# A four-layer convolution network on one Trainium2 core: a closing stage with two normalised tiles and 32-wide products, and a deformable stage normalised on ScalarE

## The reference, cut to what matters

```python
def dsc_axis(x, offset, weight, axis):        # layer 2, once along the rows, once along the columns
    ...
    s = grid_sample_zeros(x, ix, iy)
    return jnp.einsum('bchwk,ock->bohw', s, weight)

def _L3_conv_ref(x, freq_weight):             # layer 3
    kern = _equivariant_kernel(freq_weight)   # (32, 32, 3, 3)
    pad = K // 2
    return jax.lax.conv_general_dilated(x, kern, window_strides=(1, 1), padding=[(pad, pad), (pad, pad)], ...)

x = x + _L2_conv_ref(_gn(x), ...)             # ends in relu(batchnorm(...))
x = x + _L3_conv_ref(_gn(x), L3_conv_freq_weight)
```

## Time and profile before

| what | value |
|---|---|
| median of 3 runs | 4784.35 us (4765.66 to 4795.29) |
| the profiled execution, its own time | 4795.68 us |
| its span, first to last instruction | 4794.0 us |
| deformable stage, from 1992 us of the span on | 2408 us |
| closing stage, from 4407.7 us on | 386.3 us |
| granted TensorE clock, whole span | 0.878 of 2.4 GHz |

### The profile page before, as it was taken

How to read it: one execution, slowest core, us unless ns; L and a number is a source line. 1 busy time by engine, 2 the same in 40 slices (tenths; PEclk the granted TensorE clock), 3 DMA queues, 4 the chain that set the end, 5 groups by cost and what they waited for, 6 DMA issues and landing times. The chain is left out here.

```text
span 4794.0 us, 149995 instructions
## 1 busy us (share of the span) xinstructions
PE 3845.9 (80%) x58786; PEld 2247.2 (47%) x58786; DVE 2727.2 (57%) x5226; ACT 2636.6 (55%) x2855; POOL 2628.0 (55%) x1899
## 2 busy tenths in 40 slices
PE   7765558336999855399999998999989999995688
PEld 5665445232333322255555555555555555553222
DVE  4303646443333334387777777678777787775443
ACT  5500114231222244388778787788878878885332
POOL 0001200011000023499999999999989999997332
PEclk9956669658999977699999999999999999998798
DMA  3365659998777656411232212321223102222753
GB/s 97 72 125 141 190 123 261 266 303 204 215 217 213 182 185 198 79 43 26 58 66 50 55 25 57 65 49 36 49 55 68 46 29 58 54 48 77 162 136 67
DMA packets 663416, 533.27 MB, mean 111 GB/s; under 512 B 34431, under 2 KB 595711, under 8 KB 653855
## 3 DMA queue, kind: packets, MB, share of 16 engines
q1 hardware_dynamic: 544262, 386.05, 33.7%
q10 hardware_dynamic: 108560, 105.02, 7.1%
q0 software_dynamic: 9984, 33.56, 2.1%
HBM read 338.35 MB, written 186.16 MB: 109 GB/s over the span
## 5 line engine op out<-in xcount | busy, mean ns | idle before, releaser
L1576 POOL TENSOR_SCALAR df_t<-df_t 128x1536 f32<-128x1536 f32 x1536 | 2224.7, 1485 | 136.8 <-ACT df_t L1620 114.2
L1793 PE MATMUL df_o<-df_t,df_zs 128*32 128x128 f32 x36864 | 1375.0, 283 | 66.9 <-issue 55.0
L1649 DVE TENSOR_SCALAR df_t<-df_d 128x512 int32<-128x512 int32 x1536 | 1060.5, 690 | 431.2 <-PE df_d L1745 415.4
L1620 ACT ACTIVATE df_t<-df_a 128x1024 f32<-128x1024 f32 x1024 | 1050.0, 1025 | 331.1 <-PE df_a L1745 286.9
L1793 PEld LDWEIGHTS df_o<-df_t,df_zs 128*32 128x32 f32 x36864 | 942.1, 112 | 532.6 <-issue 453.9
L1745 PE MATMUL df_d<-df_ix,net_sel 11*128 11x512 bf16 x1536 | 605.3, 394 | 55.0 <-DVE df_t L1649 45.2
L1620 ACT ACTIVATE df_t<-df_z 128x1024 f32<-128x1024 f32 x512 | 524.8, 1025 | 166.6 <-PE df_z L1745 148.2
L1624 ACT ACTIVATE df_zs<-df_z 128x864 f32<-128x864 f32 x512 | 453.4, 885 | 1.5 <-PE df_z L1771 1.5
L1771 PE MATMUL df_z<-net_Z,df_x 32*128 32x288 f32 x4096 | 409.9, 458 | 0.1
L1745 PE MATMUL df_a<-df_ix,net_sel 11*128 11x512 bf16 x2048 | 406.3, 393 | 0.6 <-DVE df_s L1688 0.5
L1093 POOL CAST of_parts<-of_t_o 128x512 bf16<-128x512 f32 x64 | 39.8, 623 | 649.6 <-ACT of_t_o L1063 649.5
(11 more groups left out here) (231 smaller groups left out, 5001.8 us busy)
## 6 DMA issues: line engine op xcount, KB each, us to landing
gc_x<-x SPq DMA_DIRECT2D x240, 128.0 KB, 4.9
dc_x<-x SPq DMA_DIRECT2D x240, 128.0 KB, 3.2
dc_xt<-x_2t SPq DMA_DIRECT2D x240, 128.0 KB, 4.7
fw_x<-in_x SPq DMA_DIRECT2D x32, 512.0 KB, 6.3
iv_x<-in_x SPq DMA_DIRECT2D x64, 256.0 KB, 4.8
x<-iv_x POOLq DMA_DIRECT2D x64, 256.0 KB, 5.0
y<-gc_o ACTq DMA_DIRECT2D x64, 256.0 KB, 5.8
r_y<-y SPq DMA_DIRECT2D x8, 2048.0 KB, 14.2
```

The lines of the kernel that those rows point to most:

```text
L1576: g.tensor_scalar(t, t, 1.0, 0.0, ALU.min, ALU.max).then_inc(hat_p, 1)
L1620: act.activation(T[:, m % 2, 3 * i:3 * i + 2], src, ACT.Abs).then_inc(a_read, 1)
L1649: v.tensor_scalar(T[:, m % 2, 3 * i + 2].bitcast(I32), ps_d[:].bitcast(I32), 0x7fffffff, None, ALU.bitwise_and).then_inc(d_read, 1)
L1793: mm = pe.matmul(ps_o[32 * q:32 * q + 32, 0:P], Zs[:, m % 2, q, 32 * k:32 * k + 32], T[:, m % 2, 3 * i + x, P * q:P * q + P], start=(k == ...
```

## The change

Closing stage. The normalised image is written twice. XA has it as it lies; XB has groups 0 and 1 at row j and groups 2 and 3 at row j+1, a row of zeros at the free end. XA is written by VectorE in one piece of 4096 numbers, XB by ScalarE in two pieces of 64 partitions x 4096 (`shifted`, as scale * x + shift; the shift is -mean/deviation, two more small steps on VectorE). With these, every output row group q finds its three input rows at one offset: groups 1 and 2 in XA, group 0 in XB at row j, group 3 in XB at row j+1. So a chunk is now 3 x shifts x 4 groups = 12 products, each 128 deep, 32 wide and 512 columns long, into its own 32 partitions of the bank. The halo tiles, their copies on GpSimd and ScalarE and the products with LA and LB are gone; GpSimd only sets the two tiles to zero. The mean product now follows chunk 3, the variance product chunk 4, and on VectorE `mean` follows result 3, `variance` result 4. On ScalarE `activate(b+2)` now follows `shifted(b+1)`, and `send(b,0)` comes ahead of `root(b+1)`. L4 has the taps of all three rows for each group (12 copies), and LA and LB no longer exist.

Deformable stage. The normalising moves from VectorE to ScalarE, as scale * x + shift with the shifts of all images worked out once (NB), in the same lines 10 to 17, behind that line's `distances` and `read_z`; the eight pieces ahead of the loop move too.

The diff, cut to its core:

```diff
-        XN = s.sb("xn", [P, 2, J + 2, W + 2])
-        HA, HB = (s.sb(n, [96, 2, HJ * W]) for n in ("ha", "hb"))
+        XA = s.sb("xa", [P, 2, J, W + 2])
+        XB = s.sb("xb", [P, 2, J + 1, W + 2])
...
-                            g.tensor_copy(HA[32 * x:32 * x + 32, e].rearrange("c (j w) -> c j w", w=W),
-                                          XN[96:128, b % 2, HJ * e:HJ * e + HJ, x:x + W]).then_inc(above, 1)
+                g.memset(XA[:], 0.0).then_inc(set_, 1)
+                g.memset(XB[:], 0.0).then_inc(set_, 1)
...
-                def halo(b, e):
...
+                def shifted(b):
+                    if b == 0:
+                        a.wait_ge(set_, 2)
+                    a.wait_ge(steps, ST * (b + 1))
+                    if b >= 2:
+                        a.wait_ge(conv, NC * (b - 1))
+                    for r, j in ((slice(0, 64), 0), (slice(64, 128), 1)):
+                        a.activation(XB[r, b % 2, j:j + J, 1:W + 1], X[r, b % 3].rearrange("p (j w) -> p j w", w=W), ACT.Identity,
+                                     bias=nm[r, b % 2, 2:3], scale=nm[r, b % 2, 1:2]).then_inc(moved, 1)
...
                 for b in range(B):
+                    send(b, 0)
                     if b + 1 < B:
                         root(b + 1)
-                    send(b, 0)
-                    if b + 2 < B:
-                        a.wait_ge(added, b + 1)
-                        activate(b + 2)
                     send(b, 1)
                     if b + 1 < B:
-                        halo(b + 1, 0)
+                        shifted(b + 1)
+                    if b + 2 < B:
+                        activate(b + 2)
                     send(b, 2)
                     send(b, 3)
-                    if b + 1 < B:
-                        halo(b + 1, 1)
...
-                    for x in range(2):
-                        pe.matmul(bank[:], wt["L4"][:, x, :], XN[:, b % 2, 1 + j:5 + j, x:x + W], start=(x == 0), stop=False)
-                    if c % 4 == 0:
-                        pe.wait_ge(above, 6 * b + 3 * e + 3)
-                        pe.wait_ge(below, 6 * b + 3 * e + 3)
-                    r = slice(512 * (c % 4), 512 * (c % 4) + 512)
-                    pe.matmul(bank[0:32, :], wt["LA"][:], HA[:, e, r], start=False, stop=False)
-                    pe.matmul(bank[96:128, :], wt["LB"][:], HB[:, e, r], start=False, stop=False)
-                    pe.matmul(bank[:], wt["L4"][:, 2, :], XN[:, b % 2, 1 + j:5 + j, 2:2 + W], start=False, stop=True).then_inc(conv, 1)
+                    for x in range(3):
+                        for q in (1, 2, 3, 0):
+                            if q == 3 and x == 0 and c == 0:
+                                pe.wait_ge(moved, 2 * b + 2)
+                            r = slice(32 * q, 32 * q + 32)
+                            t, k = ((XB, j), (XA, j), (XA, j), (XB, j + 1))[q]
+                            mm = pe.matmul(bank[r, :], wt["L4"][:, x, r], t[:, b % 2, k:k + 4, x:x + W], start=(x == 0), stop=(x == 2))
+                    mm.then_inc(conv, 1)
...
# deformable, ScalarE
+                def normalise(b, a, p):
+                    if p == 0:
+                        act.wait_ge(x_in[a], 64 * (b + 1))
+                        alone(act, passed)
+                    xp = X[a][:, 512 * p:512 * p + 512]
+                    act.activation(xp, xp, ACT.Identity, bias=NB[:, bass.ds(b, 1)],
+                                   scale=GS[:, 1, bass.ds(b, 1)]).then_inc(xn, 1)
...
                         if more or m + 2 < ST:
                             ahead_of(*ahead(b, m, 2))
-
+                        if 10 <= j < 18 and (more or a == 0):
+                            normalise(*((b, 1) if a == 0 else (b + 1, 0)), j - 10)
# deformable, VectorE
-                    v.tensor_scalar(xp, xp, GS[:, 0, bass.ds(b, 1)], GS[:, 1, bass.ds(b, 1)],
-                                    ALU.subtract, ALU.mult).then_inc(xn, 1)
```

More of the change, by code:

```diff
@@ L1124, in closing @@
     NC = 8
-    HJ = J // 2
     with Stage(nc, sems, "cl") as s:
@@ L1141, in closing @@
         o_out = [s.sem(f"o_out{k}") for k in range(4)]
-        relu, added, steps, sums, rooted, normed = (s.sem(n) for n in ("relu", "added", "steps", "sums", "rooted", "normed"))
-        above, below, conv, o_done = (s.sem(n) for n in ("above", "below", "conv", "o_done"))
-        ST = 8 + 1 + 1 + 3 + 1 + 1
+        relu, added, steps, sums, rooted = (s.sem(n) for n in ("relu", "added", "steps", "sums", "rooted"))
+        normed, moved, conv, o_done = (s.sem(n) for n in ("normed", "moved", "conv", "o_done"))
+        ST = 8 + 1 + 1 + 3 + 1 + 1 + 2
         with s.block() as block:
@@ L1286, in _ @@
                         stats(b + 1)
-                    result(b, 1)
+                    for c in (1, 2, 3):
+                        result(b, c)
                     if more:
                         mean(b + 1)
-                    result(b, 2)
+                    result(b, 4)
                     if more:
                         variance(b + 1)
-                        normalise(b + 1, 0)
-                        normalise(b + 1, 1)
-                    for c in range(3, NC):
+                        normalise(b + 1)
+                    for c in range(5, NC):
                         result(b, c)
@@ L1424, in _ @@
                     r = slice(32 * q, 32 * q + 32)
[L1425 to L1430 removed]
+                    for y in range(3):
+                        t = (q - y + 1) % 4
+                        v.tensor_copy(wt["L4"][r, :, 32 * t:32 * t + 32], taps[r, y])
             @block.scalar
@@ L1723, in image @@
                             stats(b, par, c)
+                v.tensor_tensor(NB[:], GS[:, 0], GS[:, 1], ALU.mult).then_inc(shift, 1)
+                v.wait_ge(shift, 1)
+                v.tensor_scalar(NB[:], NB[:], -1.0, None, ALU.mult).then_inc(shift, 1)
                 with v.Fori(0, 1) as b:
-                    for p in range(8):
-                        normalise(b, 0, p)
                     for p in range(8):
```

69 lines of the change are left out of this document (22 added, 47 removed).

## The result

The changed kernel takes 4628.85 us (median of 4 runs, 4622.94 to 4634.74), the kernel before 4783.94 beside it (4 runs): the ratio is 0.9667, 95% interval 0.9648 to 0.9686. The profiled execution has a span of 4629.7 us, where before had 4794.0: 164.3 us less.

A forecast was written before the change was run, and what follows sets the result against it. GpSimd was taken to bound the deformable stage and a chain of waits the closing one; closing -107 and deformable -20 (-27 + 7 + 1) sum to -127 us, 4784.35 becoming 4657, range 4612 to 4720.

The forecast's parts named there:

- The head: Closing stage, its start up to the end of image 2's relu, forecast at 4479.8 us on the trace.
- The loop: Closing stage: a loop through ScalarE, addition to root, sends, two shifted writes and relu, sets 30.5 us an image.
- chunk 4 behind the wait: Closing stage: the chunk behind the mean product runs at the low clock after TensorE idles, 5.3 us.
- The chunk of 2.70: Closing stage, TensorE: twelve products as 3 sets x 2 x 0.45 us, four side by side, 2.70 us a chunk.
- first halves: Deformable stage: GpSimd's stalls around VectorE's normalising pieces go, 3.8 us an image, 27 us over images 1 to 7.
- second halves: Deformable stage: lines of 4.55 to 4.7 us against 4.30 (today 4.47), 0.7 to 1.9 us worse an image, 7 taken.
- ScalarE's line of 4.55: Deformable stage: ScalarE's 3.96 us a line plus 0.59 for the normalising piece of 512 columns.
- 60 us to win: Deformable stage, by the skill's port rule: each piece stops GpSimd for half a microsecond, 15 halves x 8 x 0.5.
- Transfers as the bound: Rival, closing stage: a round takes 38 us instead of 30.5, 37 us more, 4694 in all; chance 0.10.
- ScalarE as the bound of the deformable stage: Rival: all 128 pieces show in both halves, +56 us instead of -20, 4733 in all; chance 0.07.
- The low clock: Rival, closing stage: TensorE stays at the low clock, chunk 5.4 us, image 44.1, about 4750 in all; chance 0.05.
- Products not side by side: Rival, closing stage: a chunk takes 10.8 us, an image 87.3, 5118 in all, slower; chance 0.04.

The follow-up runs named there:

- experiment 1: Each stage's change alone: new closing stage with the old deformable function, 4674.7 us; old closing stage with the new deformable function, 4744.27 us.
- close_only: The changed kernel with the whole deformable function of the kernel before, so only the closing stage is changed: 4674.7 us, ratio 0.9758.
- quarters: The changed kernel with each of the 128 normalising pieces on ScalarE as four activations of 128 numbers instead of one of 512: 4709.63 us, ratio 0.9842.
- relu_early: The changed kernel with image b+2's relu issued behind send(b,0), ahead of root and the shifted writes: 4598.86 us, ratio 0.9607.
- relu_send: As relu_early, and send(b,1) also moved behind shifted(b+1): 4591.11 us, ratio 0.9594.
- by_quarter: The changed kernel with a chunk's twelve products reordered, the three x shifts of one group behind each other, then the next group: 4662.0 us, single run.

## Why the prediction was right, and where a term was off

The forecast was 4657 us with a range of 4612 to 4720; 4628.85 lies inside, 28 us below the forecast: -155 us between the medians against -127. Between the profiled spans it was -164.3. That parts into: closing stage -114.6; hats of the loop from first to last 2402.0 to 2346.6, -55.4; the pieces ahead of the loop +1.5; and 4.2 us by which the stages ahead, which the change does not touch, were later. Of the -55.4 some 14 come with the old loop too (experiment 1).

**Closing stage: -107 forecast, -114.6 measured.** The head was right: the relu of image 2 ends 72.0 us into the stage (4430.0), forecast 72.1. The loop had the right members in the right order. Its round was forecast as 30.5; the relus end 27.7, 30.4, 29.2, 29.3 and 30.5 us apart, 29.4 in the mean. The round shown above is the forecast's almost to a tenth: mean product 4556.90 - 4546.66 = 10.24 (10.69), root at 16.96 (17.1), relu's end at 30.4. What differs between rounds is chunk 4 behind the wait, taken as 5.3 each time; behind a wait of 1.84 us it was 2.71, and behind waits of 3.54 us 5.28, 4.04, 4.33, 5.28 and 5.28. Five rounds give 5.4 of the 7.6 us, the last eight chunks (20.9 instead of 22.9) the other 2. The chunk of 2.70 came out as 2.6.

**Deformable stage: -20 forecast, about -54 between the two profiles and -46 between medians, and here is the term that was mis-sized.** In first halves the forecast was -27; lines 12 to 19 lost 298.2 - 266.4 = 31.8 (28.8 against `close_only`). The eight pieces ahead of the loop were forecast at +1 and cost 1.5. The step that failed is "In second halves 4.55 to 4.7 against 4.30 (today 4.47): 0.7 to 1.9 us worse than today an image, seven times, 7 taken". Lines 44 to 51 got 15.0 us shorter (12.6 against `close_only`), 22 from the forecast. Two things are behind it. ScalarE's line of 4.55 was a sum of lengths; by starts the line is 4.32, although the piece itself lasts 0.81 and not 0.59, and `quarters` shows that starts are what count. So the line stayed at GpSimd's pace, 240.5 / 56 = 4.29: 7 x 8 x (4.47 - 4.29) = 10 us. And 4.47 was read from image 3 alone: it holds in five of the seven images (35.7 us for the eight lines), but in images 1 and 2 the first pieces stall GpSimd in second halves too (39.1 and 37.8); these 5.4 us went as well. Two signs that the prediction named did not come: the line of 4.5 to 4.6 us in second halves, and a stage of 2380 to 2395 us, which is 2365.9. A further 8.6 us (of which 7.5 in lines 34 to 43) lie in lines of the loop that the forecast did not treat; kernels with the same loop differ there by as much.

**The two statements on GpSimd and VectorE.** I went by the rows and against the page (the Trainium skill, SBUF — State Buffer, "Who interferes with whom"), by which whoever comes first holds the ports for its whole instruction; my estimate from that was 60 us to win. Measured were 31.8 + 15.0 = 46.8 in the lines with pieces (41.4 against `close_only`), between the two. One new row speaks for the page. VectorE now works out the shifts NB, 8 numbers per partition, while GpSimd sets a tile to zero:

```profile
1950.39 13.75 POOL L1584 MEMSET df_ix<- 128x16384 bf16 x1 [18.41 <-POOLq L1019]
1950.72 0.17 DVE L1713 TENSOR_TENSOR df_nb<-net_GS 128x8 f32<-128x8 f32 x1 [17.87 <-PEq L1019]
1950.92 13.24 DVE L1715 TENSOR_SCALAR df_nb<-df_nb 128x8 f32<-128x8 f32 x1
```

The tensor_scalar of 8 numbers lasts 13.24 us and ends with the memset: it waited for the whole instruction. It costs nothing here, since the loop's first tile is not in before 1984.

**The rivals.** *Transfers as the bound* fell: `relu_early` and `relu_send` make them go faster than after does. *ScalarE as the bound of the deformable stage* fell for after, and `quarters` shows it as it was meant, 0.8 us per line further on. *The low clock* fell as a bound of the whole stage (0.86, up from 0.83); what it costs shows in chunk 4, up to 5.28 us instead of 2.71. *Products not side by side* fell, and even in the order of `by_quarter` three ran side by side.

## What to carry to other kernels

ScalarE, running back to back, is timed by the distance between starts, not by the sum of lengths: here 4.32 against 4.78 us a line, and against a bound of 4.30 that turned a forecast loss into a gain. A product that waits for another engine belongs behind as much independent work as there is: moved ahead by three chunks, it left TensorE idle 11.3 us instead of 3.5 an image and cost 60 us. Behind a wait TensorE can pay a second time (a chunk of up to 5.28 us behind 3.54 us idle, 2.71 behind 1.84). When a chain through one engine is the bound, look at what stands on it without need: moving one relu ahead of two copies, with no change of the work, gave another 30 us, and the best kernel of the study is `relu_send`, 4591.11 us.

## What the runs showed that was not expected

- A VectorE operation of 8 numbers per partition took 13.24 us beside a GpSimd memset of 13.75 us, while another of 0.17 us passed at the memset's start.
- On VectorE neither an odd count (511) nor a stride of two changed the time per number (0.5 ns), and a form with two input tensors (0.75 us for 512) waited beside GpSimd like the others, up to 5.38 us.
- ScalarE needed 0.48 us for 128 numbers and 0.81 for 512, in place and in a row 0.39 and 0.70 apart; 1024 numbers out of PSUM took 1.02 and stood 0.90 apart. A small piece is mostly fixed cost.
- TensorE ran products of three quarters side by side even when they were issued quarter by quarter (a chunk every 3.56 us instead of 2.6), with less overlap just before a product of full width.
- In the closing stage the DMA engines moved up to 282 GB/s over 30 us, where I had taken 234 for their most, from the closing stage of the kernel before.
